# Clearing two DRAM buffers in pieces of 1.6 KB, with three matrix pieces instead of six in the first stage and the chunk marks loaded last

## The reference, cut to what matters

```python
# layer 0: typed graph attention, two sublayers, edges sorted by dst
k, q, v = typed_linear(x, ntype, Wk), typed_linear(x, ntype, Wq), typed_linear(x, ntype, Wv)
kT = einsum('nhd,htdo->nhto', k, Watt)      # a table row for each node and relation
vT = einsum('nhd,htdo->nhto', v, Wmsg)
a  = (kT[src, :, etype] * q[dst]).sum(-1) * pri[:, etype].T / sqrt(16)
att = edge_softmax(a, dst, n)               # softmax over the edges of one dst
hag = segment_sum(vT[src, :, etype] * att, dst)
...
# layers 1 and 3 need sum over edges of h[src] into dst; the kernel computes it
# as a product with the count matrix C[src, dst]
```

## Time and profile before

| | |
|---|---|
| median of three runs | 3,843.22 us (3,835.6 to 3,844.84) |
| the profiled execution, its own time | 3,847.27 us |
| its span in the trace | 3,845.6 us |
| granted TensorE clock, mean | 0.776 of full speed |
| stage `idx` | to 154.8 us |
| stage `qkv0` | 154.8 to 306.0 us |
| stage `tab0` | 306.0 to about 624 us |

### The profile page before, as it was taken

How to read it: one execution, slowest core, us unless ns; L and a number is a source line. 1 busy time by engine, 2 the same in 40 slices (tenths; PEclk the granted TensorE clock), 3 DMA queues, 4 the chain that set the end, 5 groups by cost and what they waited for, 6 DMA issues and landing times. The chain is left out here.

```text
span 3845.6 us, 42073 instructions
## 1 busy us (share of the span) xinstructions
PE 2610.9 (68%) x11696; PEld 1711.6 (45%) x11696; DVE 1813.0 (47%) x4239; ACT 1122.4 (29%) x2928; POOL 2202.2 (57%) x1985
## 2 busy tenths in 40 slices
PE   1537992666662658992666663638968888859696
PEld 1325662555551335662555552334444444434343
DVE  6524442555562455442555552431058888830303
ACT  0113440222221743440222222730034555510001
POOL 4316557777777876557777777860047777720000
PEclk9966555888876875555788786868969999969797
DMA  9988996898975448996898884447546666547372
GB/s 350 310 339 320 395 391 155 259 266 263 268 224 109 73 120 306 396 391 169 255 263 261 267 235 94 92 133 235 194 117 192 188 187 190 153 169 271 123 272 85
DMA packets 656434, 872.83 MB, mean 227 GB/s; under 512 B 120594, under 2 KB 540761, under 8 KB 615653
## 3 DMA queue, kind: packets, MB, share of 16 engines
q1 hardware_dynamic: 298564, 567.61, 42.0%
q0 software_dynamic: 120320, 158.13, 18.0%
q10 hardware_dynamic: 237360, 144.89, 12.3%
HBM read 441.21 MB, written 429.28 MB: 226 GB/s over the span
## 5 line engine op out<-in xcount | busy, mean ns | idle before, releaser
L1698 POOL DMA_INDIRECT att_rows<-table,kvrow x784 | 797.4, 1017 | 247.6 <-issue 232.8
L1465 POOL DMA_INDIRECT matrix<-count,place x392 | 620.0, 1582 | 255.1 <-DMA matrix<-count,place 185.9
L2101 POOL DMA_INDIRECT msg_rows<-rows,msg_src x392 | 404.0, 1031 | 338.1 <-DMA msg_src<-in_src_pt 218.9
L1756 PE MATMUL att_po<-att_message,att_mate 128*128 128x264 f32 (+1 forms) x1568 | 394.5, 407 | 10.8 <-ACT att_out L1824 5.4
L1548 DVE COPY tab_part<-tab_bank 128x512 f32<-128x512 f32 x400 | 257.5, 686 | 294.4 <-DMA table<-tab_part 276.3
L1589 PE MATMUL tab_bank<-wk,tab_kv 32*128 32x256 f32 x1600 | 363.9, 696 | 30.5 <-DVE tab_part L1548 19.2
L1725 PE MATMUL att_pq<-a,att_mate 128*128 128x128 f32 x1152 | 215.2, 347 | 223.3 <-DVE att_prod L1882 222.8
L1756 PEld LDWEIGHTS att_po<-att_message,att_mate 128*128 128x128 f32 x1568 | 305.9, 238 | 65.2 <-DVE att_message L1933 26.2
L1882 DVE TENSOR_TENSOR att_prod<-att_rows,att_pq 128x512 f32<-128x512 f32 x196 | 134.8, 688 | 424.0 <-DMA att_rows<-table,kvrow 423.6
L1589 PE MATMUL tab_bank<-wv,tab_kv 32*128 32x256 f32 x1600 | 332.2, 618 | 0.0
L1573 ACT ACTIVATE tab_part<-tab_bank 128x512 f32<-128x512 f32 x400 | 221.7, 594 | 312.8 <-DMA table<-tab_part 297.8
(11 more groups left out here) (403 smaller groups left out, 4147.2 us busy)
## 6 DMA issues: line engine op xcount, KB each, us to landing
table<-tab_part SPq DMA_DIRECT2D x200, 1024.0 KB
gsum_cells<-matrix SPq DMA_DIRECT2D x50, 1604.0 KB
att_sums<-att_out ACTq DMA_DIRECT2D x196, 272.0 KB
matrix<-a SPq DMA_DIRECT2D x25, 1604.0 KB
nb_cells<-matrix SPq DMA_DIRECT2D x25, 1604.0 KB
a<-query_rows SPq DMA_DIRECT2D x144, 256.0 KB
query_rows<-a SPq DMA_DIRECT2D x16, 1568.0 KB
att_message<-in_ea_rows SPq DMA_DIRECT2D x98, 256.0 KB, 4.6
```

The source lines that it names most:

```text
L1465: nc.gpsimd.indirect_dma_start(D.matrix, bass.IndirectOffsetOnAxis(ap=K.place[:, col:col + 1], axis=0), K.count[:, col:col + 1], None, com ...
L1698: nc.gpsimd.indirect_dma_start(rows[g % RR][:, j, :], None, D.table, bass.IndirectOffsetOnAxis(ap=K.kvrow[:, t:t + 1], axis=0)).then_inc(r ...
L1756: nc.tensor.matmul(po[j][:, 0:w], mate[h % RS][:, j, :], message[h % RM][:, j, 0:w], start=True, stop=True).then_inc(summed, 1)
L2101: nc.gpsimd.indirect_dma_start(rows[g % RR][:, j, :], None, D.rows, bass.IndirectOffsetOnAxis(ap=src[:, t:t + 1], axis=0)).then_inc(rows_i ...
```

## The change

Every clearing transfer moves the same bytes, but in 1,024 pieces instead of 128: a partition's run is cut in eight, and the source names the same eighth of the zeroed tile eight times. A piece of `query_rows` is 392 numbers (1,568 bytes), one of the matrix 402 numbers (1,608 bytes). So that the width divides by eight, a matrix row has 16 spare columns instead of 8, of which the product still uses 8. The first stage clears three row blocks instead of six, the second stage 22 instead of 19, and there the chunk marks are loaded after the clearing instead of ahead of it.

```diff
-AW = NP + STREAMS
+AW = NP + 16
+STRIP = AW // 8
...
-EARLY_WIPES = 6
+EARLY_WIPES = 3
...
             for i in range(PIECES):
-                sp.dma_start(rows[:, i * WIPE:(i + 1) * WIPE], K.zero[:, 0:WIPE]).then_inc(K.cleared, 16)
+                sp.dma_start(rows[:, i * WIPE:(i + 1) * WIPE].rearrange("p (b c) -> p b c", b=8),
+                             K.zero[:, 0:WIPE // 8].unsqueeze(1).broadcast_to([P, 8, WIPE // 8])).then_inc(K.cleared, 16)
...
     for i in rows:
-        sp.dma_start(cells[i], K.zero[:, 0:AW]).then_inc(K.wiped, 16)
+        sp.dma_start(cells[i].rearrange("p (b c) -> p b c", c=STRIP),
+                     K.zero[:, 0:STRIP].unsqueeze(1).broadcast_to([P, AW // STRIP, STRIP])).then_inc(K.wiped, 16)
...
             if l == 0:
+                wipe_matrix(nc, K, D, sp, range(EARLY_WIPES, NT))
                 load_chunks(nc, K, D, sp)
-                wipe_matrix(nc, K, D, sp, range(EARLY_WIPES, NT))
...
-                last = nc.tensor.matmul(ext[0:STREAMS, 0:P], cells[i % R][:, NP:AW], rows[:, i, :], start=i == 0, stop=i == NT - 1)
+                last = nc.tensor.matmul(ext[0:STREAMS, 0:P], cells[i % R][:, NP:NP + STREAMS], rows[:, i, :], start=i == 0, stop=i == NT - 1)
```

## The result

The changed kernel took 3,853.11 us in the median of 18 runs (3,842.14 to 3,862.72), the kernel before 3,842.92 us in 18 runs beside them (3,835.6 to 3,847.62): ratio 1.0031, 95% interval 1.0022 to 1.0040. It is slower by 10 us; the forecast was 15 us faster, range 3,811 to 3,850. The profiled execution has a span of 3,848.7 us.

A forecast was written before the change was run, and what follows sets the result against it. The prediction took full DMA engines, with short transfers waiting behind long clearing packets, to bound the early stages. Gains of 10 and 6 us gave 3,847.3 - 16.3 + 1 = 3,832 us profiled, 3,828 us for the median; range 3,811 to 3,850.

The forecast's parts named there:

- turns by packet: Clearing beside stores: engines take one packet of each queue in turn, so 1.5 KB stores wait for 12.8 KB clearing packets.
- the sum: Engine time added up per stage: 110 us of work from 32 us on in the first, 134 us in the second.
- equal counts: Sign in the profile after: q1 and q10 again equal between 170 and 190 us, several times as many in 10 us.
- SP's presence at the barrier: Second stage: SP must issue everything before the barrier, so it stays until the clearing is all but drained, done at +141.5.
- The price of a piece: Clearing in both stages: 66 ns a packet for both sizes, floor 61, ceiling 80; 4.29 us a transfer.
- ragged pieces: Rival on clearing pieces off round addresses: 4.6 ns more a packet, 12 us, so 3,840; chance 0.17.
- The rival "slower": Clearing on q1: short DRAM writes not beginning or ending on a whole line cost 80 ns or more; 3,865 at 80; chance 0.13.
- The rest of `degree`, 1 us: First stage, from 32 us on: what remains of the `degree` store on ACT's queue, taken as 1 us of engine time.
- First stage: Clearing 81.5 us plus other transfers; ends at 144.5 instead of 154.8, 10 us gained.
- Second stage: Clearing 94.4 us plus stores, loads and gathers; takes 145.2 us instead of 151.2, 6 us gained.
- the break-even of 72 ns: Clearing packets on q1: each ns is 2.7 us; at 72 ns the gain is gone, from 76 measurably slower.
- The Trainium skill's rule: Clearing pieces starting off 256 bytes: an estimated 128 bytes more paid for each; the prediction saw no sign in the trace.

## Why the prediction was wrong

The mechanism stood, turns by packet and full engines. What failed was the price of a packet, in two terms of the sum: a matrix piece cost 84 to 88 ns where the sum had 66, and `degree` 9 us where it had 1.

- **Turns by packet: right.** Before, q1 and q10 had equal counts; after, they have 754 and 752 between 132 and 137 us. In the second stage, where I had looked for equal counts, q1 has more (684 and 556 between 205 and 210 us), since q10 is at times empty: ACT waits for PE there and no longer for its stores. The gathers start 70 us into the stage (forecast +65), ACT's and PE's chain is off the path. That the path is SP's presence at the barrier was only half right: with the chunk marks first SP leaves earlier and POOL waits for the drain instead.
- **The price of a piece: the step that failed.** "I take 66 ns for both sizes" was 1.4 ns low for the query rows and 19 ns low for matrix pieces alone on the engines. Of the 19 ns some 13 belong to the borders; the other 6 stay with good borders too (71.5 to 72.5 ns), and no run explains them. It was extrapolated from packets whose borders are multiples of 16 bytes, every one of them: the 528-byte rows which I took as proof against ragged pieces are 33 times 16, and reads. The experiments put the 13 ns down to neighbours written in succession whose common border is not such a multiple. The rival "slower" had named 80 ns or more, for a whole line not filled; its price came, with this narrower cause. Beside the stores of the second stage the matrix pieces are cheap (64.5 ns a packet of either queue); beside `hx` they are not (106 ns a pair against 88).
- **degree: mis-sized.** "The rest of `degree`, 1 us" was 9. I had taken its busy share for its cost. In turn with clearing pieces a 4-byte store took an estimated 45 ns of an engine, and the queue drained in 30 us, not 15. In the kernel before half of these ran in the tail, at 14 ns.
- **First stage.** Forecast end 144.5, measured 157.8. `degree` explains 8 us; 1,040 query packets an engine at 67.4 instead of 66 ns, 1.5 us; 195 matrix packets an engine at 84 instead of 66 ns, 3.5 us: 13.0 of 13.3. Transfers landed 4.5 to 5 us after the end of their issue, not 3, so `hx` was issued at 126.9 (forecast 123.5), which costs nothing while the engines are full.
- **Second stage.** Forecast 145.2 us, measured 157.5. The clearing drained 149.9 us after its start instead of 135.5. From 260 to 307.7 us some 8,650 matrix packets went nearly alone at 83 ns instead of 66, 9.2 us; 5 us are spread over the mixed stretches and not resolved. The chunk marks then held SP for 6.3 us (forecast 6), and the barrier took 1.4 us, not 3.7.
- **Together** the third stage came 25.6 us later than forecast, 9.3 after the kernel before; the rest of the kernel only shifted. With neighbours kept apart it starts at 301.0, with borders on multiples of 16 at 304.9 and 306.1, where the kernel before has 306.0 on its own chip. So the borders decided between slower and about even, as the break-even of 72 ns said, and even good borders do not give the 15 us of the forecast. The chance of 0.14 on the slow side was too small for a price extrapolated from other packets.
- **The Trainium skill's rule** weighed in the prediction ("DMA: Bandwidth & Descriptors", section "How a descriptor splits into AXI transactions": a start off 256 bytes is paid from the boundary below) would charge the same pieces at the same addresses alike. It is not what went wrong: 1,608-byte pieces cost 84.1 ns with their neighbours in turn and 71.5 without. Whether it has a part in the other 6 ns no run here shows, since every piece size tried starts mostly off a multiple of 256.

## What to carry to other kernels

DMA queues take turns by packet, so the size of a background transfer's packets sets how long every short transfer beside it takes: cut it where others wait, leave it long where nobody does, and count what the short pieces cost the engines, from packets of the same size and the same borders. When a contiguous run is cut, put the cuts on multiples of 16 bytes, or keep neighbouring pieces from following each other. And look for the consumer's real first need: with one wait moved behind 25 scatters that do not depend on it, the end of the clearing ran under them.

## What the hardware showed unexpectedly

DRAM writes of 1.6 KB that follow their neighbours cost 84 to 88 ns of an engine each where every other border lies 8 bytes beyond a multiple of 16, and 71 to 73 ns with all borders on multiples of 16 or with the neighbours in different transfers. Stores of 4 bytes took an estimated 45 ns of an engine in turn with clearing pieces and 14 ns almost alone. SP could run about 78 long packets an engine ahead, 14 MB in all. Of short ones it was about 135 when its last matrix piece was accepted at 295.7, only 3.4 MB: the room in the queue goes by packets far more than by bytes.
